# The projection stage of a cross-attention and feed-forward kernel, rebuilt: order of the transposes, place of the sums, weight pieces, context blocks

## The chip, the cores and the metric

One core of a Trainium2 chip. The metric is the device time of one execution in microseconds (us). Engines are named as in the profile: TensorE (PE, with its weight loads PEld), VectorE (DVE), ScalarE (ACT), GpSimd (POOL) and SyncE (SP), which here only issues transfers.

## The reference

```python
# x (1, 4096, 512), ctx (1, 3202, 1024), W_in (512, 512), w1 (512, 2048), w2 (2048, 512), all float32
h  = rmsnorm(layernorm(x), g_res) @ W_in.T + b_in
hp = rmsnorm(ctx, g_init)[:, :512]
s  = scan(hp)                    # s[i] = A' * s[i-1] + exp(-0.001) * hp[i], a first-order recurrence
plug = clip(cumsum(boundary_mask) - 1, 0, 3201)    # boundary_mask from cumsum(mask)
x  = x + h + s[plug]
y  = layernorm(x)
x  = x + gelu(y @ w1 + b1) @ w2 + b2
```

Everything is float32. The kernel keeps that accuracy by splitting each matmul operand into a high and a low part of type float32r and taking three products (high by high, low by high, high by low).

## The kernel before

x is cut into 32 tiles of 128 rows; four tiles make a group (8 groups). There are two stages.

**The projection stage** makes x1 = x + h for each tile and stores it to DRAM (x1_dram). For tile t, `tile_stats` (DVE) takes mean and variance, `tile_scale` (POOL) makes scale and bias, `tile_norm` (ACT) writes the normalized rows to `na`, `transpose_first` (PE) puts four 128x128 transposes into one of two PSUM banks `t_bank`, `tile_high` (ACT) and `tile_low` (DVE) split them into `h_hi` and `h_lo` (two buffers each), `project` (PE) makes twelve 128x512 matmuls into one of four banks `acc`, `tile_add` (DVE) adds x and writes to one of two buffers `xb`, and SP stores `xb`. PE's order is: transposes of tile t+1, projection of tile t. x arrives in eight buffers `xa`, six tiles ahead. `tile_add` waits until the store of the tile two before has landed (`xb_stored`, line 934).

The context is handled in seven blocks of 512 rows. Three of them (NA = 3) are handled in the projection stage, one in each span of eight tiles: SP loads both halves (1 MB each), ACT takes squares (`squares`), POOL makes the scale (`context_scale`) and multiplies by g_init (`times_g_init`), ACT scales the rows (`scale_rows`), DVE scans over four rows (`scan_row`), a small banded product on PE (`carry`) carries the state across partitions, DVE adds it (`add_carry`), and SP stores the block into `table` in DRAM (`store_block`). The mask is turned into row numbers (`plug`) by DVE and PE in the first span.

The weights w1 (four chunks of 128 rows of K) and w2 (four chunks) are loaded whole, chunk by chunk, by ACT and SP (1 MB each). ACT makes `w_hi` (line 678), POOL `w_lo` (`low_weights`, line 478), in 128x512 pieces. The last pieces are made after the projection stage.

**The feed-forward stage (FFN)** handles group by group. For group g, POOL has gathered s[plug] by an indirect transfer into `x_next` on top of x1 + b_in (`add_bias`, `add_context`, lines 494 and 499); DVE takes statistics (`second_stats`) and normalizes (`second_norm`, line 1062), PE transposes (`transpose_second`, line 825), ACT and DVE split (`transposed_high`, `transposed_low`), all for group g+1 during the last steps of group g. The 16 steps m of a group are on PE: `ffn1(g, m)` (12 matmuls), then `ffn2(g, m-2)` (12 matmuls). A step's gelu is on ACT (h_hi and g_f32), its split on DVE. Groups 0 to 3 also handle context blocks 3 to 6. The preparation of group 0 is the end of the projection stage.

Each engine runs its own program in order; semaphores are all that links them. The order inside an iteration is written out by hand.

Of the kernel before, what the change touches and what calls it, by code (L numbers as in the profile page):

```python
# [30 lines left out]
P = 128  # L31
# [8 lines left out]
PT = 8  # L40
NPAIR = NT // PT
AHEAD = PT - 2
LEAD = 2
# [5 lines left out]
NA = 3  # L49
# [48 lines left out]
def xattn_ffn(nc, x, ctx, mask, w_in, b_in, g_res, g_init, w1, b1, w2, b2, out):  # L98
# [4 lines left out]
    w1_v = w1.rearrange("(k p) n -> k p n", p=P)  # L103
# [6 lines left out]
    with es:  # L110
# [28 lines left out]
        win_hi = place("win_hi", [P, K, D], F32R, offset=xt_at)  # L139
        win_lo = place("win_lo", [P, K, D], F32R, offset=xt_at + 8 * KB)  # L140
# [15 lines left out]
        xa = place("xa", [P, PT, D], F32, offset=w_hi_at + 6 * WC * 4)  # L156
# [15 lines left out]
        ch_all = place("ch_all", [P, R, D], F32, offset=n_rows_at)  # L172
        scan_in = place("scan_in", [P, R, D], F32, offset=w_lo_at + 7 * WC * 4)
        scan_out = place("scan_out", [P, R, D], F32, offset=w_lo_at + 6 * WC * 4)
        xb = place("xb", [P, 2, D], F32, offset=x_cur_at)
        na = place("na", [P, 2, D], F32, offset=x_cur_at + 4 * KB)
# [14 lines left out]

        st_a = sb("st_a", [P, PT, 6])
        mv_a = sb("mv_a", [P, PT, 2])
        va_a = sb("va_a", [P, PT])
        ra = sb("ra", [P, PT])
        na_bias = sb("na_bias", [P, PT])
# [34 lines left out]
        acc = [bank(f"acc{i}") for i in range(TI)]  # L231

# [5 lines left out]
        xa_loaded = [sem(f"xa_loaded{i}") for i in range(PT)]  # L238
        xb_stored = [sem(f"xb_stored{i}") for i in range(2)]
        w_loaded = [sem(f"w_loaded{i}") for i in range(WCH)]  # L240
        cl_loaded = sem("cl_loaded")
        ch_all_loaded = sem("ch_all_loaded")
# [31 lines left out]
        w_lo_done = sem("w_lo_done")  # L274
        w2_ready = sem("w2_ready")
        sq_done = sem("sq_done")
# [23 lines left out]
        def _(sp):  # L300
            sp.dma_start(xa[:, 0, :], x_v[0, :, 0, :]).then_inc(xa_loaded[0], 16)
# [8 lines left out]
            for t in range(1, AHEAD):  # L310
                sp.dma_start(xa[:, t, :], x_v[t // TI, :, t % TI, :]).then_inc(xa_loaded[t], 16)

            def load_rows(b, dst, cols, loaded):

                if isinstance(b, int) and b == 0:
                    p = ZEROS // R
                    n = R - ZEROS % R
                    sp.dma_start(dst[p:p + 1, R - n:R, :], ctx_v[0:n, cols].rearrange("(p j) d -> p j d", p=1))\
                        .then_inc(loaded, 16)
                    sp.dma_start(dst[p + 1:P, :, :], ctx_v[n:BLK - ZEROS, cols].rearrange("(p j) d -> p j d", j=R))\  # L320
                        .then_inc(loaded, 16)
                else:
                    rows = ctx_v[bass.ds(block_start(b), BLK), :].rearrange("(p j) d -> p j d", j=R)
                    sp.dma_start(dst, rows[:, :, cols]).then_inc(loaded, 16)

            def load_low_half(b):

                load_rows(b, cl[:], slice(0, D), cl_loaded)

            def load_high_halves(b):  # L330

                load_rows(b, ch_all[:], slice(D, DG), ch_all_loaded)

            def load_high_half(b, j):

                wait_apart(sp, sq_done, R * b + j - 1)
                rows = ctx_v[bass.ds(block_start(b), BLK), :].rearrange("(p j) d -> p j d", j=R)
                sp.dma_start(ch[:, j % 2, :], rows[:, j, D:DG]).then_inc(ch_loaded[j % 2], 16)
# [6 lines left out]
            def tile(h, t, more=True):  # L345

                h, t = h + t // PT, t % PT
                if not isinstance(h, int) or PT * h + t > 0:
                    wait_apart(sp, acc_read, PT * h + t)
                    v = (t - 1) % PT  # L350
                    g = 2 * h + (t - 1) // TI
                    sp.dma_start(x1_dram[g, :, v % TI, :], xb[:, v % 2, :]).then_inc(xb_stored[v % 2], 16)
                if more:
                    u = (t + AHEAD) % PT
                    g = 2 * h + (t + AHEAD) // TI
                    sp.dma_start(xa[:, u, :], x_v[g, :, u % TI, :]).then_inc(xa_loaded[u], 16)

            def load_late_weights(c):

                sp.dma_start(w_raw[:, c, :].rearrange("p (m n) -> p m n", m=4), w2_v[c - 4, :, :, :])\  # L360
                    .then_inc(w_loaded[c], 16)

            def span(h, last=False):
                first = isinstance(h, int) and h == 0
                for s in range(PT - LEAD if last else PT):
                    if s == 7 and not first:
                        store_block(h - 1, scan_out)
                    if s == 5 and last:
                        store_block(h - 1, scan_in)
                    tile(h, LEAD + s, more=not last)  # L370
                    if s == 0 and not last:
                        if first:
                            wait_apart(sp, zeroed, 2)
# [832 lines left out]
```

## Time and profile before

| | us |
|---|---|
| median of 3 runs | 908.57 |
| lowest, highest | 906.12, 911.9 |
| span of the profiled execution | 907.9 |
| that execution's own device time | 909.6 |
| PE busy in the span | 847.1 (93%) |
| DVE, ACT, POOL busy | 329.9, 292.7, 285.2 |

Busy time is summed over the instructions of an engine; for PE the ends are modelled and matmuls overlap, so the distance between the starts of matmuls says more than the duration of one. Times of the trace are counted from the start of the span. An instruction's row may end in the idle time of its engine before it and in the one that ended that idle time.

### The profile page before, as it was taken

The numbers are of one execution on the slowest core, as the hardware profiler recorded it, in microseconds if no ns is written. First come the engines' busy times: TensorE is split into PE (matmuls) and PEld (weight loads), VectorE is DVE, ScalarE is ACT, GpSimd is POOL, SyncE is SP. The second block draws the span as 40 slices with busy tenths as digits, with TensorE's granted clock in tenths as the row PEclk, the third lists the DMA queues.
The fourth block names the chain that finished last, engine by engine and source line by source line (L and its number), as shares of the span: only waits on it lengthen the run. The fifth ranks groups of instructions, "written<-read, shape, count | busy, mean of one in ns | idle before, by whom it ended". The sixth has DMA issues, their size and how long they took to land.

```text
span 907.9 us, 11322 instructions
## 1 busy us (share of the span) xinstructions
PE 847.1 (93%) x3781; PEld 696.2 (77%) x3781; DVE 329.9 (36%) x531; ACT 292.7 (32%) x505; POOL 285.2 (31%) x323
## 2 busy tenths in 40 slices
PE   5688787379999999999999999999999999999998
PEld 4576665268888888888888888888888888888886
DVE  4766565351444144314431443213221322232112
ACT  3375562034323431343234322223222222222221
POOL 4275564491822070217022603400430043002000
PEclk8898997879999999999999999999999999999999
DMA  7956745432124131403140312300220032001001
GB/s 221 300 194 209 238 148 181 100 128 70 24 67 132 55 45 46 162 23 46 45 162 23 46 45 93 47 1 1 92 46 0 0 102 36 0 0 47 1 1 46
DMA packets 34414, 73.14 MB, mean 81 GB/s; under 512 B 5548, under 2 KB 6572, under 8 KB 31984
## 3 DMA queue, kind: packets, MB, share of 16 engines
q1 hardware_dynamic: 25124, 57.34, 18.8%
q0 software_dynamic: 4608, 8.39, 6.3%
q10 hardware_dynamic: 4656, 7.09, 2.5%
q8 instruction: 13, 0.21, 0.1%
q14 instruction: 13, 0.11, 0.0%
HBM read 48.92 MB, written 23.89 MB: 80 GB/s over the span
## 4 chain that ended last, share of the span: by engine, by line
PE 81%; DMA 7%; DVE 4%; POOL 4%; issue 2%; ACT 1%; ACTq 1%; SPq 1%; POOLq 0%; DVEq 0%
PE acc L781 13%; PE acc L782 13%; PE acc L783 13%; PE h_bank L781 13%; PE h_bank L782 13%; PE h_bank L783 13%; DMA x_part<-xb 3%; PE t_bank L825 2%; DMA x_next<-scan_table,idx 1%; DMA x_next<-x_part 1%; DMA g_init_b<-in_L_xattn_g_init_dram 1%; DMA xa<-in_x_dram 1%; POOL cl L505 1%; DVE h_lo L926 1%; POOL x_next L494 1%
## 5 line engine op out<-in xcount | busy, mean ns | idle before, releaser
L1146 DVE TENSOR_TENSOR h_lo<-g_f,h_hi 128x512 fp32r<-128x512 f32 x128 | 111.9, 874 | 441.1 <-ACT g_f L744 441.1
L742 ACT ACTIVATE h_hi<-h_bank,b_c 128x512 fp32r<-128x512 f32 x128 | 88.3, 690 | 453.9 <-PE h_bank L783 453.9
L781 PE MATMUL h_bank<-xt_hi,w_hi 128*128 128x512 f32 x512 | 200.7, 392 | 1.5 <-DVE xt_lo L1067 1.5
L781 PE MATMUL acc<-w_hi,h_hi 128*128 128x512 f32 x512 | 200.0, 391 | 0.0
L782 PE MATMUL h_bank<-xt_lo,w_hi 128*128 128x512 f32 x512 | 199.9, 390 | 0.0
L783 PE MATMUL h_bank<-xt_hi,w_lo 128*128 128x512 f32 x512 | 199.8, 390 | 0.0
L783 PE MATMUL acc<-w_hi,h_lo 128*128 128x512 f32 x512 | 199.4, 389 | 0.0
L782 PE MATMUL acc<-w_lo,h_hi 128*128 128x512 f32 x512 | 199.2, 389 | 0.0
L781 PEld LDWEIGHTS h_bank<-xt_hi,w_hi 128*128 128x128 f32 x512 | 96.6, 189 | 21.7 <-ACT xt_hi L725 1.9
L783 PEld LDWEIGHTS h_bank<-xt_hi,w_lo 128*128 128x128 f32 x512 | 96.6, 189 | 20.1
L782 PEld LDWEIGHTS h_bank<-xt_lo,w_hi 128*128 128x128 f32 x512 | 96.6, 189 | 19.8
L783 PEld LDWEIGHTS acc<-w_hi,h_lo 128*128 128x128 f32 x512 | 96.1, 188 | 20.0
L781 PEld LDWEIGHTS acc<-w_hi,h_hi 128*128 128x128 f32 x512 | 96.1, 188 | 20.0 <-issue 0.3
L782 PEld LDWEIGHTS acc<-w_lo,h_hi 128*128 128x128 f32 x512 | 96.2, 188 | 19.8
L584 POOL TENSOR_TENSOR x_cur<-x_next,b_b 128x512 f32<-128x512 f32 x32 | 47.8, 1524 | 159.1 <-DMA out_dram<-x_cur 158.9
L744 ACT ACTIVATE g_f<-h_bank,b_c 128x512 f32<-128x512 f32 x128 | 87.4, 683 | 2.1 <-DVE h_lo L1146 2.1
L781 PE MATMUL acc<-win_hi,h_hi 128*128 128x512 f32 x128 | 58.6, 458 | 9.5 <-DVE h_lo L926 9.5
L494 POOL TENSOR_TENSOR x_next<-x_next,b_in_b 128x512 f32<-128x512 f32 x32 | 54.1, 1690 | 22.8 <-DMA x_next<-x_part 22.2
L499 POOL DMA_INDIRECT x_next<-scan_table,idx x32 | 53.3, 1666 | 25.1 <-POOL x_next L494 25.1
L509 POOL TENSOR_SCALAR va_b<-mv_b 128x4 f32<-128x4 f32 x8 | 1.6, 195 | 172.9 <-DVE mv_b L1053 172.9
L782 PE MATMUL acc<-win_lo,h_hi 128*128 128x512 f32 x128 | 55.3, 432 | 0.0
L783 PE MATMUL acc<-win_hi,h_lo 128*128 128x512 f32 x128 | 54.8, 428 | 0.0
(133 smaller groups left out, 694.8 us busy)
## 6 DMA issues: line engine op xcount, KB each, us to landing
xa<-in_x_dram SPq DMA_DIRECT2D x32, 256.0 KB, 5.9
x_part<-xb SPq DMA_DIRECT2D x32, 256.0 KB, 3.7
x_next<-x_part SPq DMA_DIRECT2D x8, 1024.0 KB, 4.8
out_dram<-x_cur SPq DMA_DIRECT2D x32, 256.0 KB, 2.1
w_raw<-in_L_ffn_w_dram ACTq DMA_DIRECT2D x6, 1024.0 KB, 9.8
cl<-in_ctx_dram SPq DMA_DIRECT2D x6, 1024.0 KB
ch<-in_ctx_dram SPq DMA_DIRECT2D x16, 256.0 KB, 2.7
scan_table<-cl SPq DMA_DIRECT2D x4, 992.0 KB
```

The source lines that it names most:

```text
L494: step(pool.tensor_tensor(v, v, b, ALU.add))
L499: pool.indirect_dma_start(x_next[:, i, :], None, rows, bass.IndirectOffsetOnAxis(ap=idx[:, i:i + 1].bitcast(U32), axis=0), compute_op=ALU. ...
L505: pool.tensor_tensor(cl[:, j, :], cl[:, j, :], g_init_b[:], ALU.mult).then_inc(g_scaled, 1)
L584: ins = pool.tensor_tensor(x_cur[:, i, :], x_next[:, i, :], b2_b[:], ALU.add)
L742: act.activation(h_hi[:, m % HB, :], h_bank[m % 2][:], ACT.Gelu, bias=b1_c[:, m:m + 1])
L744: act.activation(g_f32[:], h_bank[m % 2][:], ACT.Gelu, bias=b1_c[:, m:m + 1]).then_inc(gelu_done, 1)
L781: nc.tensor.matmul(dst, a_hi, b_hi, start=first, stop=False)
L782: nc.tensor.matmul(dst, a_hi, b_lo, start=False, stop=False)
L783: return nc.tensor.matmul(dst, a_lo, b_hi, start=False, stop=final)
L825: ins = nc.tensor.transpose(t_bank[i % 2][:, k * P:(k + 1) * P], n_rows[:, i, k * P:(k + 1) * P], ident[:])
L926: dve.tensor_tensor(h_lo[:, t % 2, :], t_bank[t % 2][:], h_hi[:, t % 2, :].bitcast(F32), ALU.subtract).then_inc(t_lo, 1)
L1146: dve.tensor_tensor(h_lo[:, m % HB, :], g_f32[:], h_hi[:, m % HB, :].bitcast(F32), ALU.subtract).then_inc(h_split, 1)
```

## The change

- **Transposes two tiles ahead.** PE's order becomes: transposes of tile t+2, projection of tile t. The transposes use four banks (`t_bank` 0 and 1, `acc` 2 and 3), the projections only `acc` 0 and 1. `h_hi` and `h_lo` have four buffers, the normalized rows go to `n_rows` (four). The loops over spans are written out, all 32 tiles.
- **Sums in place.** `tile_add` writes into the tile of x; x has 16 buffers (`xa_even`, `xa_odd`), loaded 13 tiles ahead. SP stores from there, and waits for the store of tile t-3 before it loads tile t+13 over it. `xb` is gone.
- **Statistics six tiles ahead**, scales for two tiles in one set of four operations (`scales`).
- **Weights.** w1 comes in four pieces of 512 columns, all K, instead of four chunks of 128 rows; w2 as before. w1 pieces 0 and 1 and w2 chunk 0 are split in the projection stage; w2(1), w1(2), w2(2), w1(3), w2(3) by ACT in group 0 of the FFN, with the low parts on POOL, those of w1(3) and w2(3) on DVE. Five of the eight loads move to SP, at t = 25, 27, 29 and after the last tile.
- **Context.** Two blocks (NA = 2) in the projection stage; blocks 2 to 6 in FFN groups 0 to 4, at earlier steps of a group (squares from step 1, scan at 7, carry at 8, store after 9). The block's table entries are then gathered in the same group.
- **FFN preparation.** Group 0's four gathers come one after the other at t = 23; its norms at t = 28 to 30, its transposes at t = 30 and 31. In each group the second statistics are at steps 12 and 13, all four norms at step 14.
- **Order at the start.** The clears of `cl` and `ch_all` stand behind the scales of tile 0, `band` is made later, the mask's preparation is spread over t = 0 to 12. g_init, b_in and b2 are loaded ahead of b1 and of the weights.

The core of the diff (waits and unchanged neighbours cut):

```diff
-PT = 8
-NPAIR = NT // PT
-AHEAD = PT - 2
-LEAD = 2
+XR = 16
+SR = 4
-NA = 3
+NA = 2
...
+        xa_even = place("xa_even", [P, XR // 2, D], F32, offset=xt_at)
+        xa_odd = place("xa_odd", [P, XR // 2, D], F32, offset=w_hi_at + 6 * WC * 4)
+        first_bank = [t_bank[0], t_bank[1], acc[2], acc[3]]
...
+            for t in range(1, 6):
+                load_tile(t)
+            wait_apart(sp, zeroed, 2)
+            load_first_rows(ch_all, slice(D, DG), ch_all_loaded)
+            load_first_rows(cl, slice(0, D), cl_loaded)
+            for t in range(6, XR):
+                load_tile(t)
+            for t in range(NT):
+                if t > 0:
+                    store_x1(t - 1)
+                if t >= 3:
+                    wait_x1(t - 3)
+                    if t - 3 + XR < NT:
+                        load_tile(t - 3 + XR)
+                if t == 4:
+                    sp.dma_start(cl_next[:], block_rows(1)[:, :, 0:D]).then_inc(cl_next_loaded, 16)
+                if t == 8:
+                    wait_apart(sp, sq_done, R)
+                    sp.dma_start(ch_all[:], block_rows(1)[:, :, D:DG]).then_inc(ch_all_loaded, 16)
+                if t == 15:
+                    store_block(0, cl)
+                if t == 17:
+                    wait_apart(sp, table_stored, STORED + 16)
+                    load_low_half(NA)
+                if t == 19:
+                    sp.dma_start(x_next[:], x1_dram[0, :, :, :]).then_inc(x_next_loaded, 16)
+                if t == 22:
+                    store_block(1, cl_next)
+                    load_high_half(NA, 0)
+                    load_high_half(NA, 1)
+                if t == 25:
+                    wait_apart(sp, table_stored, STORED + 16 * 2)
+                    load_w2(1)
+                if t == 27:
+                    load_w1(2)
+                if t == 29:
+                    load_w1(3)
...
# POOL
+            scales(0, 1)
+            pool.memset(cl[:], 0.0).then_inc(zeroed, 1)
+            pool.memset(ch_all[:], 0.0).then_inc(zeroed, 1)
+            scales(1, 1)
+            scales(2, 2)
...
+            for t in range(NT):
+                if t % 2 == 0 and t + 6 < NT:
+                    scales(t + 6, 2)
+                if t == 3:
+                    pool.wait_ge(small_loaded, 16 * 4)
...
+                if t == 23:
+                    wait_apart(pool, table_stored, STORED + 16 * 2)
+                    for i in range(TI):
+                        add_context(0, i, 2)
...
# PE
-                if not isinstance(n, int) or n >= TI:
-                    pe.wait_ge(acc_read, n - TI + 1)
+                if t >= 2:
+                    pe.wait_ge(acc_read, t - 1)
...
+            transpose_first(0)
+            transpose_first(1)
+            for t in range(NT):
+                if t + 2 < NT:
+                    transpose_first(t + 2)
...
+                if t == 30:
+                    transpose_second(0, 0)
+                    transpose_second(0, 1)
+                if t == 31:
+                    transpose_second(0, 2)
+                    transpose_second(0, 3)
+                project(t)
...
# DVE
-                if not isinstance(n, int) or n >= 2:
-                    dve.wait_ge(xb_stored[t % 2], 16 * (PT // 2 * h + t // 2))
-                dve.tensor_tensor(xb[:, t % 2, :], acc[t % TI][:], xa[:, t, :], ALU.add).then_inc(acc_read, 1)
+                dve.tensor_tensor(xa(t), acc[t % 2][:], xa(t), ALU.add).then_inc(acc_read, 1)
...
+            for t in range(NT):
+                if t > 0:
+                    tile_add(t - 1)
+                if t + 2 < NT:
+                    tile_low(t + 2)
+                if t == 0:
+                    mask_parts()
+                if t + 6 < NT:
+                    tile_stats(t + 6)
+                if t == 2:
+                    mask_positions()
+                if t == 3:
+                    mask_places()
+                    one_hots_q()
+                if t == 4:
+                    one_hots_p(0, MJ // 2)
+                if t == 5:
+                    one_hots_p(MJ // 2, MJ)
...
+                if t == 31:
+                    for i in range(TI):
+                        transposed_low(0, i)
+            tile_add(NT - 1)
```

## Rows read from the trace of the kernel before

**Rows 1.** The page's slices: PE's busy tenths in 40 equal slices.

```profile
PE   5688787379999999999999999999999999999998
```

**Rows 2.** Stage table: stretch, length, busy us (instructions) by engine, PE clock, DMA share, GB/s.

```profile
0.00:191.00 191.00, 133.47 (x586) 104.92 (x587) 111.82 (x223) 84.04 (x141) 101.53 (x172) 0.85 0.63 194
63.00:76.00 13.00, 12.93 (x64) 10.44 (x64) 8.92 (x17) 8.18 (x10) 6.56 (x15) 1.00 0.73 254
191.00:196.00 5.00, 5.00 (x16) 3.95 (x16) 0.00 (x0) 1.09 (x2) 5.00 (x5) 0.67 0.83 276
```

**Rows 3.** Timeline of PE: start us, us, instruction, [idle before, what ended it].

```profile
15.34 0.79 PE L781 MATMUL acc<-win_hi,h_hi 128*128 128x512 f32 x1 [1.16 <-DVE h_lo L926]
...
20.46 0.60 PE L777 MATMUL t_bank<-ident,na 128*128 128x128 f32 x4
...
33.66 1.11 PE L777 MATMUL t_bank<-ident,na 128*128 128x128 f32 x4 [5.39 <-ACT na L630]
...
63.07 0.65 PE L777 MATMUL t_bank<-ident,na 128*128 128x128 f32 x4 [2.89 <-DVE h_lo L926]
...
72.72 0.60 PE L777 MATMUL t_bank<-ident,na 128*128 128x128 f32 x4
...
181.65 1.12 PE L825 MATMUL t_bank<-ident,n_rows 128*128 128x128 f32 x4 [12.94 <-DVE n_rows L1062]
...
190.61 0.77 PE L781 MATMUL h_bank<-xt_hi,w_hi 128*128 128x512 f32 x1 [1.50 <-DVE xt_lo L1067]
```

**Rows 4.** Table of waits: who waited for whom, us in total, times, longest.

```profile
DVE xb L935 <- DMA x_part<-xb: 16.9, 5, 4.9
...
POOL va_a L467 <- DMA g_init_b<-in_L_xattn_g_init_dram: 10.6, 1, 10.6
```

**Rows 5.** Chain of work that ended last, stretch 0 to 230: start us, us, what.

```profile
67.93 9.00 DMA x_part<-xb
...
93.60 13.47 DMA x_part<-xb
...
164.72 12.80 DMA x_next<-scan_table,idx
```

**Rows 6.** Timeline of DVE, and two of its groups by line (count, busy, mean ns).

```profile
26.27 0.17 DVE L990 CAST fa<-ia 128x26 f32<-128x26 int32 x1
...
28.43 0.18 DVE L1001 CAST pos_q<-ib 128x26 f32<-128x26 int32 x1
...
68.50 0.69 DVE L926 TENSOR_TENSOR h_lo<-t_bank,h_hi 128x512 fp32r<-128x512 f32 x1 [0.40 <-ACT h_hi L644]
...
70.61 0.71 DVE L941 SCALAR_TENSOR_TENSOR scan_in<-scan_in 128x512 f32<-128x512 f32 x1
...
269.06 1.00 DVE L1062 TENSOR_SCALAR n_rows<-x_next,mv_b,rb 128x512 f32<-128x512 f32 x2
...
L945 DVE CAST l_hi<-scan_in 128x512 fp32r<-128x512 f32 x3 | 3.9, 1291 | 0.0
L1005 DVE TENSOR_TENSOR oh_p<-pos_p,iota_p 128x1664 bf16<-128x1664 f32 x2 | 3.8, 1881 | 0.0
```

**Rows 7.** Groups of POOL by line, 0 to 191 us: count, busy, mean ns, idle before.

```profile
L478 POOL TENSOR_TENSOR w_lo<-w_raw,w_hi 128x512 fp32r<-128x512 f32 x15 | 20.0, 1401 | 0.0
L469 POOL TENSOR_TENSOR ra<-va_a,neg_half 128x1 f32<-128x1 f32 x32 | 17.7, 552 | 4.8 <-POOL va_a L467 0.8
...
L478 POOL TENSOR_TENSOR w_lo<-w_raw,w_hi x8 | 10.2, 1281 | 0.0
L499 POOL DMA_INDIRECT x_next<-scan_table,idx x4 | 6.7, 1666 | 3.3 <-POOL x_next L494 3.3
...
L461 POOL MEMSET cl<- 128x2048 f32 x1 | 1.8, 1804 | 0.2 <-POOL band L456 0.2
```

**Rows 8.** Timeline of ACT with its issues (ACTq), and its weight copies by line.

```profile
18.55 3.85 ACTq L674 DMA_DIRECT2D b_in_b<-in_L_xattn_b_in_dram  x1
...
L678 ACT ACTIVATE w_hi<-w_raw (+1 forms) x7 | 13.3, 1901 | 0.0
```

**Rows 9.** DMA issues, 0 to 192 us: count, median us from issue to landing.

```profile
x_next<-scan_table,idx POOLq DMA_INDIRECT x4, 5.5
```

More of the change, by code:

```diff
@@ L391, in _ @@
-            sp.sem_inc(table_stored, STORED)
-            for t in range(LEAD):
-                tile(0, t)
-            span(0)
-            with sp.Fori(1, NPAIR - 1) as h:
-                span(h)
-            span(NPAIR - 1, last=True)
-            wait_apart(sp, acc_read, NT)
-            sp.dma_start(x1_dram[NG - 1, :, TI - 1, :], xb[:, 1, :]).then_inc(xb_stored[1], 16)
-            wait_apart(sp, table_stored, STORED + 16 * NA)
-            load_late_weights(7)
-            for s in xb_stored:
-                wait_apart(sp, s, 16 * NT // 2)
@@ L412, in group @@
+            store_x1(NT - 1)
+            load_w2(2)
+            load_w2(3)
+            for t in range(NT - SR, NT):
+                wait_x1(t)
+            def group(g, scan, more, prep):
                 if prep:
@@ L551, in _ @@
-            tile_scale(0, 0)
-            tile_scale(1, 1)
-            tile_scale(2, 2)
-            tile_scale(3, 3)
-            pool.wait_ge(small_loaded, 16 * 4)
-            span(0)
-            with pool.Fori(1, NPAIR - 1) as h:
-                own.looped(h, 1, 2 * PT + 3)
-                span(h)
-            own.left(NPAIR - 2)
-            span(NPAIR - 1, last=True)
-            for q in range(4):
-                low_weights(4, q, 6, w2_ready)
-            low_weights(3, 2, 6, w_lo_done)
@@ L704, in _ @@
-            tile_norm(0, 1)
-            tile_high(0, 0)
-            first_loads(0)
-            tile_high(1, 1)
-            tile_norm(0, 2)
-            first_loads(1)
-            span(0)
-            act.wait_ge(counted, 1)
-            for c in range(1, 6):
-                act.wait_ge(w_loaded[c], 16)
-            with act.Fori(1, NPAIR - 1) as h:
-                own.looped(h, 1, R)
-                span(h)
-            own.left(NPAIR - 2)
-            span(NPAIR - 1, last=True)
-            act.sem_inc(gelu_done, CREDIT)
@@ L751, in group @@
                     transposed_high(g + 1, 3)
-            with act.Fori(0, NB - NA) as g:
-                own.looped(g, 0, R)
+            group(0, True, True)
+            with act.Fori(1, NB - NA) as g:
+                own.looped(g, 1, R)
                 group(g, True, True)
-            own.left(NB - NA)
+            own.left(NB - NA - 1)
             with act.Fori(NB - NA, NG - 1) as g:
@@ L890, in group @@
                         ffn2(g, m - LAG)
[L891 removed]
+                    if scan and m == 8:
                         carry(NA + g, t_bank[0][:])
@@ L1122, in _ @@
-            tile_low(0, 0)
-            tile_stats(0, 2)
-            tile(0, 1)
-            mask_positions()
-            span(0)
-            with dve.Fori(1, NPAIR - 1) as h:
-                own.looped(h, 1, PT + R)
-                span(h)
-            own.left(NPAIR - 2)
-            span(NPAIR - 1, last=True)
-            for i in range(TI):
-                second_norm(0, i)
-            tile_add(NPAIR - 1, PT - 1)
-            dve.wait_ge(h_used, NT)
-            for i in range(TI):
-                transposed_low(0, i)
+            tile_stats(0)
@@ L1139, in group @@
+            tile_add(NT - 1)
             def group(g, scan, prep):
+                first = isinstance(g, int) and g == 0
                 for m in range(M):
```

716 lines of the change are left out of this document (353 added, 363 removed).

## The prediction

> **What bounds the kernel now.** I read the page's slices first. TensorE (PE) is full in the last thirty of them; all holes lie in the first nine [rows 1]. The stage table gives them a size: in the first 191 us PE is busy for 133.5, at a mean granted clock of 0.85 [rows 2]. The feed-forward stage (FFN) begins with the h_bank matmul at 190.61 us [rows 3] and runs to the end of the span, 907.9: 717.3 us in which PE waits for nothing worth naming. So the change is worth what it does to the first 190.6 us.
>
> What would they cost without waits? The transposes that open a tile start at 63.07 and, three tiles on, at 72.72 [rows 3]: 3.22 us a tile, of which twelve matmuls at 0.23 are 2.76 and the transposes 0.46. 32 tiles are 103 us, and the first product begins at 15.34 [rows 3]. Some 70 us are therefore waiting, low clock and tail. The table of waits and the chain name them:
> - A sum waits for a store. DVE xb waits 16.9 us in five waits [rows 4], and the chain shows single stores landing after 9.00 and 13.47 us [rows 5]. They share SyncE's (SP) queue with the 1 MB transfers of the context blocks, and only two xb buffers lie between them and PE.
> - GpSimd (POOL) waits 10.6 us for g_init before the scales of tile 4 [rows 4], so PE waits for that tile's norm: after a tile that ended near 28 the next transpose comes at 33.66, 5.39 us late and at low clock [rows 3].
> - The tail. The fourth gather of group 0 lands 12.80 us after its issue [rows 5], and PE waits 12.94 us for the norms [rows 3].
>
> **The change, part by part.** T(t) is the moment at which PE turns to tile t, which now opens with the transposes of tile t+2.
>
> *Sums into the tile of x.* xb and its wait are gone. A slot of x is reused only after 16 tiles, and SP issues loads 13 tiles ahead for statistics that run 6 ahead: 7 tiles, 22.5 us, of cover against the worst store seen (13.47). I price the store waits at nothing; without that cover they are the 16.9 us again. What comes next is the sum itself: acc has two banks instead of four, so project(t+1) waits for the add of tile t-1. That add can start when project(t-1) ends and must be done before project(t+1) starts: 3.22 us plus 0.4 of transposes, less 0.6 for the add, so some 2.9 us of lateness are allowed.
>
> *The budget of VectorE (DVE).* One tile costs it h_lo, statistics, aggregate and add: 68.50 to 70.61, 2.11 us [rows 6]. That leaves 1.1 us a tile for lumps. Eleven small mask operations take 2.4 us (26.27 to 28.6 [rows 6]): one such set at t=2, one with the one-hot q (half an one-hot p, 1.0) at t=3, and one-hot p twice 1.88 at t=4 and 5 [rows 6]. Lateness runs 1.3, 3.6, then +0.8 and +0.8; what exceeds 2.9 is PE waiting: 0.7+0.8+0.8. Block 0 at t=11 is three scan rows (0.7, as at 70.61), a cast of 1.29 [rows 6] and a subtract of 0.7: 4.1 us; then the plug (six small ones, 1.4) and two carry steps of 1.3: +0.1, +0.4, +0.2, +0.2. Block 1's lumps (t=17 to 21) stay under. In sum 3 us. Bound below: 0. Bound above: no lateness allowed at all. Then 32 x 2.11, 36 for all lumps and second statistics and 0.4 us a tile of waiting for ACT's copy are 116 us against PE's 103: 13 us. In [rows 6] a tile with a scan row in it still kept to 3.2 us, so I stay near the low end.
>
> *Two tiles ahead: the start.* project(0) now stands behind transpose_first(2), thus behind the statistics of tiles 2 and 3, their scales and the norm of tile 2. POOL clears cl and ch_all (1.80 us each [rows 7]) after scales(0), so norm(1) ends near 14.2; h_hi 0.6, h_lo 0.6 and two statistics of 0.85 make 17.1. Scales for two tiles: four small operations and a power; one power of one column takes 0.55 [rows 7], of two columns between that and 1.1, I take 0.7; with the hops 1.9: 19.0. Norm 0.8, first transposes: project(0) at about 20.7, 5.4 us later than now (bounds: 18, if the clears and scales overlap better, and 23). Its 12 matmuls follow a long idle, so at 1.2 GHz like those from 15.34 to 20.46: 5.1 us [rows 3]. In return the gap before 33.66 goes: g_init is issued first, and POOL asks for it only at t=3, near 32 us. One ACT issue took 3.85 us right behind the many small pieces of b1 [rows 8]; b1 now goes last, in front of a weight load. Between 0 and 3.85 us; the two tiles of lead hide it, I take 0.
>
> *Weights in pieces.* 8 subtracts of w1 and 4 of w2 stay in the stage; at 1.28 to 1.40 us [rows 7] that is 16 us of POOL, and with scales, context and gathers it stays under 80 of the 103. ACT's copies of 1.90 us [rows 8] at t=7, 14 and 18 go with high (0.6) and norm (0.8): 3.3 us against 3.22. w2(1), w1(2), w1(3), w2(2) and w2(3) are split in group 0 of the FFN, where ffn1 and ffn2 of a step take 24 x 0.23 = 5.5 us. POOL there: 6 us for x_cur, 4 x 1.4 for w2(1), the context, and 4 x 1.4 for w1(2) until 39 us into the stage; needed at step 8, 44. Bias and w2(2) until 50; needed behind ffn1(10), 58. DVE's subtracts at steps 10 and 11 are done 6 us after ffn1(10), needed 8 after. Price 0; uncovered, each late chunk costs up to 5 us.
>
> *Two blocks instead of three first.* 2 MB of loads, 1 MB of store and 8 us of DVE leave the stage. In each FFN group all norms move to step 14: a norm takes 0.50 [rows 6] and stands between h_lo and transposes that PE is ready for at about that time: 0 to 0.5 us for each of 7 groups; 0.3 makes 2. The FFN no longer starts at the low clock (granted 0.67 from 191 to 196 [rows 2]), which gives 5 x 0.33 = 1.7 back. The FFN stays at 717.3.
>
> *The tail.* Block 1 is ready near T(22)+1. Its 1 MB store: 194 GB/s at a share of 0.63 [rows 2] is 308 GB/s at full share, 3.4 us, with issue and receipt 5. Four gathers back to back, 1.67 each [rows 7], end at T(22)+12.8; landing takes 5.5 at the median [rows 9]: T(27)+2.2, where DVE wants the last one at T(27)+2.4. No slack. Bounds: 0, and 10 if store or gather meet the delays of [rows 5]; most landings are near the median, I take 2. At t=31 the second pair of second transposes asks for xt_lo, which DVE makes after project(30) and its add: 0.6+0.7+0.1, then 0.7, less one transpose: 1.7 us.
>
> **Sum.** 20.7 start + 5.1 first tile + 31 x 3.22 = 99.8 + 4.4 for counts, mask totals, two carries (three matmuls each) and four transposes + 3 DVE + 1.7 + 2 tail = 136.7 us, against 190.6. With 717.3: a span of 854.0. The median of the runs, 908.57, lies 0.7 above the profile's span, so **855 us**.
>
> **Rivals.**
> - *As summed* (0.57): a pitch of 3.2 to 3.4 us; own range 845 to 864.
> - *The transfers crowd the tail* (0.22). For it: the stage still moves some 33.5 MB (191 us at 194 GB/s are 37 today), 109 us at 308 GB/s of its 130. The table store, the gathers and three weight loads meet at t=22 to 29, and POOL scales tiles 30 and 31 only after it has issued the gathers. Against: no x loads are left after t=18. 8 to 18 us more: 863 to 873. The Trainium skill (DMA: Bandwidth & Descriptors, "Queues, rings and completion order") says that an engine's semaphore write lands only after its earlier writes of all queues; the late stores of [rows 5] agree.
> - *DVE becomes the bound* (0.14). 10 to 13 us more than summed: 860 to 871.
> - *A weight chunk is late in group 0* (0.04): 5 to 20 us, 860 to 875.
> - *The clock stays low* (0.03), the other side. If DVE's short delays kept PE at 1.2 GHz throughout, a tile would be 12 x 0.43 + 1.1 = 6.2 us, the stage 20.7 + 198 + 8 = 227, the end 944. Slower begins at a pitch of 5.1. For it: 0.85 granted today, and 33.66. Against: 1.00 in the stretch of full tiles [rows 2]. The Trainium skill (TensorE: Matmul & The Clock Gate, "What's actually happening") calls the throttled clock the default that activity lifts; 15.34 and 33.66 agree.
>
> **The numbers.** The range runs from a start of 18 with nothing for DVE and tail (847), less 4 for terms that I rounded up (843), to the crowded tail with half of DVE's upper bound (880). About 1% is what a measurement tells from no change. Faster 0.95, within 1% 0.02, slower 0.03: only the last rival ends above.
>
> **What will show it.** First h_bank matmul near 137 us; transposes every 3.2 to 3.4 us from t=6 to t=29; no DVE wait on a store; clock 1.00 after 26 us; an FFN of 717. Wrong if PE waits for DVE's adds at most tiles, if st_b waits over 3 us for a gather, or if PE waits inside group 0.

## The result: the changed kernel is 2% slower

| | before | after |
|---|---|---|
| median of four runs, us | 909.1 (906.12 to 911.9) | 926.97 (925.03 to 929.68) |
| span of the profiled execution, us | 907.9 | 926.8 |
| first product (PE acc) | 15.34 | 20.76 |
| start of the FFN (first h_bank product of group 0) | 190.61 | 167.18 |
| from there to the end | 717.3 | 759.6 |

The ratio of the medians is 1.0199, with an interval of 1.0154 to 1.0244: the kernel did get slower, but whether by more or by less than 2% stays open. The forecast was 855 us. The projection stage did become shorter, by 23.4 us and not by 53.9. The FFN, whose time I had left as it was, became 42.3 us longer. 42.3 - 23.4 is the 18.9 us by which the two spans differ.

The slices of the page show both. First the row of PE, then the group of instructions of the page in which PE's new wait stands (busy time, mean ns of one, idle time just before and what ended it):

```profile
PE   3988895998799998999799979998999999999998
...
L831 PE MATMUL t_bank<-ident,n_rows 128*128 128x128 f32 x128 | 20.6, 312 | 30.1 <-DVE n_rows L1063 28.5
```

In [rows 1] the last thirty slices were full. Now a 7 or 8 comes back every fourth or fifth slice up to the twenty-eighth. The stage table puts sizes to it. Its columns are those of [rows 2]: the stretch and its length, PE, PEld, DVE, ACT and POOL, the granted clock, the DMA share and GB/s. The first row is group 0 of the FFN, the second is group 1, the third is a late group without a scan:

```profile
167.00:256.00 89.00, 80.64 (x350) 66.33 (x349) 32.76 (x45) 35.68 (x55) 37.88 (x31) 0.95 0.29 86
256.00:354.00 98.00, 91.73 (x405) 75.94 (x405) 29.50 (x45) 30.32 (x56) 26.70 (x23) 0.97 0.22 64
736.00:826.00 90.00, 89.93 (x405) 74.35 (x405) 21.67 (x36) 22.33 (x36) 19.34 (x15) 1.00 0.14 35
```

A group that scans a block lasts 98 us and a group that doesn't lasts 90, with the same 405 matmuls. The holes are at one place in each group. On PE's timeline (start, duration, line, tiles, count, and in brackets the wait before it) they stand at the transposes of the next group's rows, here of groups 1 and 2:

```profile
254.22 1.97 PE L831 MATMUL t_bank<-ident,n_rows 128*128 128x128 f32 x8 [5.48 <-DVE n_rows L1063]
351.89 1.96 PE L831 MATMUL t_bank<-ident,n_rows 128*128 128x128 f32 x8 [6.27 <-DVE n_rows L1063]
```

The other three are at 450.32 (6.40), 549.23 (6.64) and 645.30 (3.71). The table of waits tells what n_rows waited for. Each row is who waits for whom, the sum, the count and the longest wait:

```profile
PE t_bank L831 <- DVE n_rows L1063: 28.5, 5, 6.6
DVE st_b L1053 <- DMA x_next<-scan_table,idx: 63.0, 16, 13.3
POOL x_next L509 <- DMA scan_table<-cl: 160.0, 5, 34.0
```

Read upwards: POOL holds back the gathers until the store of the block has landed, DVE's statistics wait for the gathers, and PE waits for the norms. The chain of waits shows the store and the gather behind it (start and duration):

```profile
120.37 15.57 DMA scan_table<-cl_next
...
223.48 12.98 DMA scan_table<-cl
242.92 7.67 DMA x_next<-scan_table,idx
...
320.53 12.96 DMA scan_table<-cl
```

The store of one block takes 12.98 us. I had priced it at 5. And it takes this in the quiet FFN, with no crowd about it. The stage table of the stretch around the store of 223.48:

```profile
224.00:236.00 12.00, 12.00 (x55) 9.94 (x54) 6.20 (x10) 5.16 (x7) 0.00 (x0) 1.00 0.23 85
```

The share of the 16 DMA engines is 0.23 while nothing else of size moves, as if a quarter of them worked. The kernel before makes the same store, and its trace has nearly the same share in a stretch that the prediction did not use, just behind the issue at 260.9:

```profile
262.00:273.00 11.00, 11.00 (x54) 9.18 (x53) 3.60 (x8) 2.16 (x4) 1.24 (x2) 1.00 0.25 91
```

There the gathers of the next group did not need the block just stored, so nobody waited. The change moves two blocks out of the projection stage, and the gathers for group g+1 now need the block that group g makes. That puts the store on the path.

### The profile page after: what moved, and what is told of

Same layout as the page of the kernel before. It is cut to its first block, busy times and chain, and to the rows that moved or that the text cites. A ratio compares the mean times of both kernels' runs of the same rounds, so it can differ in the third digit from the quotient of the medians.

```text
span 926.8 us, 10866 instructions
## 1 busy us (share of the span) xinstructions
PE 852.5 (92%) x3781; PEld 701.8 (76%) x3781; DVE 320.3 (35%) x539; ACT 293.9 (32%) x506; POOL 265.6 (29%) x286
## 3 DMA queue, kind: packets, MB, share of 16 engines
q1 hardware_dynamic: 26756, 60.49, 19.3%
## 4 chain that ended last, share of the span: by engine, by line
PE 67%; DMA 15%; DVE 8%; POOL 5%; issue 3%; ACT 1%; DVEq 0%; ACTq 0%; POOLq 0%; SPq 0%
PE acc L788 11%; PE acc L790 11%; PE acc L789 11%; PE h_bank L788 10%; PE h_bank L789 10%; PE h_bank L790 10%; DMA scan_table<-cl 7%; DMA x_next<-scan_table,idx 5%; POOL x_next L509 3%; PE t_bank L831 2%; DMA scan_table<-cl_next 2%; DVE cl L957 1%; DVE st_a L929 1%; DMA x_part<-xa_even 1%; DVE cl L946 1%
## 5 line engine op out<-in xcount | busy, mean ns | idle before, releaser
L1146 DVE TENSOR_TENSOR h_lo<-g_f,h_hi 128x512 fp32r<-128x512 f32 x128 | 102.4, 800 | 425.6 <-ACT g_f L730 420.7
L788 PE MATMUL h_bank<-xt_hi,w_hi 128*128 128x512 f32 x512 | 203.0, 396 | 0.0
L790 PEld LDWEIGHTS h_bank<-xt_hi,w_lo 128*128 128x128 f32 x512 | 97.5, 190 | 20.7
L509 POOL DMA_INDIRECT x_next<-scan_table,idx x32 | 50.8, 1587 | 176.0 <-DMA scan_table<-cl 160.0
L831 PE MATMUL t_bank<-ident,n_rows 128*128 128x128 f32 x128 | 20.6, 312 | 30.1 <-DVE n_rows L1063 28.5
L504 POOL TENSOR_TENSOR x_next<-x_next,b_in_b 128x512 f32<-128x512 f32 x32 | 43.2, 1350 | 15.8 <-DMA x_next<-x_part 11.6
```

Source lines behind the costliest of these rows:

```text
L504: step(pool.tensor_tensor(x_next[:, i, :], x_next[:, i, :], b_in_b[:], ALU.add))
L509: pool.indirect_dma_start(x_next[:, i, :], None, rows, bass.IndirectOffsetOnAxis(ap=idx[:, i:i + 1].bitcast(U32), axis=0), compute_op=ALU. ...
L788: nc.tensor.matmul(dst, a_hi, b_hi, start=first, stop=False)
L790: return nc.tensor.matmul(dst, a_lo, b_hi, start=False, stop=final)
L831: ins = nc.tensor.transpose(t_bank[i % 2][:, k * P:(k + 1) * P], n_rows[:, i, k * P:(k + 1) * P], ident[:])
L1146: dve.tensor_tensor(h_lo[:, m % HB, :], g_f32[:], h_hi[:, m % HB, :].bitcast(F32), ALU.subtract).then_inc(h_split, 1)
```

## The experiments

**Theory A**: the block store is slow because its 124 partitions are spread over 4 of the 16 DMA engines, and this store is what PE waits for in the FFN and in the tail. **Rival B**: the four gathers in a row and all norms at step 14 are the cost (the chain behind the store is too long, however fast the store is). **Rival C**: the store is slow on its DRAM side, however it is cut.

The projection stage has a loss of its own. By the prediction's sum the transposes of tile 29 start near 115.2; they started at 133.73, 18.5 us later. **Theory D**: PE's carry, which stands ahead of the products of tiles 12 and 19 and waits for DVE, and the waits for norms near it have taken them. **Rival E**: VectorE is simply full.

Each quoted expectation was written before its run.

**1. The same store, cut where 16 engines share it.** 112 of the 124 partitions in one transfer, 12 in a second; the waits count 32 for a block and no longer 16. Bytes, order and dependences are the same.

```
     wait_apart(sp, block_ready, b + 1)
-    sp.dma_start(table[bass.ds(STEP * b, STEP), :].rearrange(...), src[HP:P, :, :]).then_inc(table_stored, 16)
+    sp.dma_start(table[bass.ds(STEP * b, 112 * R), :].rearrange(...), src[HP:HP + 112, :, :]).then_inc(table_stored, 16)
+    sp.dma_start(table[bass.ds(STEP * b + 112 * R, 12 * R), :].rearrange(...), src[HP + 112:P, :, :]).then_inc(table_stored, 16)
...
-    wait_apart(pool, table_stored, STORED + 16 * blocks)
+    wait_apart(pool, table_stored, STORED + 32 * blocks)
```

> The changed kernel with one edit: each block store of 124 partitions is issued as two, of 112 and of 12 partitions. Theory A (the store is slow, 12.95 us for 992 KB at a DMA share of 0.23, because a transfer of 124 partitions is spread over 4 of the 16 DMA engines, and since the gathers now wait for the block of their own group the wait reaches PE): the store lands in 4 to 6 us, POOL's wait for it shrinks by 8 us in each of groups 0 to 4, PE's waits for n_rows in the FFN (28.5 us) go to under 3, the FFN takes 718 to 722 instead of 759.6, the first stage loses about 8 of its 167; span 876 to 884. Theory B (the four gathers in a row and all norms at step 14 are what costs, the store only stands in front of them): the store may be faster, but PE still waits in each group; the FFN stays above 740, the span above 900. Theory C (the store is slow on its DRAM side, however it is cut): nothing changes, 925 to 929.

Measured: 879.6 us against 908.27, a ratio of 0.9679 (0.9657 to 0.9702). The FFN starts at 157.38 and lasts 720.7. From the timelines of SP and POOL, the issue of the store and the first gather that waited for it, and the stage table between them:

```profile
212.32 0.37 SPq L342 DMA_DIRECT2D scan_table<-cl  x1
...
217.77 1.68 POOL L511 DMA_INDIRECT x_next<-scan_table,idx  x1 [14.42 <-DMA scan_table<-cl]
...
212.50:217.50 5.00, 5.00 (x24) 4.14 (x23) 3.06 (x5) 3.08 (x3) 0.00 (x0) 1.00 0.61 203
```

From issue to gather it is 5.4 us, at a share of 0.61. PE has no wait for n_rows in the FFN any more. One edit of one transfer is worth 47.4 us, 38.9 of them in the FFN. A holds, and C falls.

**2. The dependence taken away, the store left slow.** The gathers read a table that is one block shorter. For the mask used here all rows asked for lie in it; for another mask this kernel would be wrong.

```
-    wait_apart(pool, table_stored, STORED + 16 * 2)
+    wait_apart(pool, table_stored, STORED + 16 * 1)
...
-        add_context(0, i, 2)
+        add_context(0, i, 1)
...
-    blocks = NA + g + 1 if scan else NB
+    blocks = NA + g if scan else NB
```

> The changed kernel, but each gather reads and waits for a table one block shorter (for this mask all rows asked for lie in it), so a block's store has a whole group of time, as in the kernel before. Theories A and C (the wait for the store is the cost): FFN 717 to 722, PE never waits for n_rows there, span 874 to 884. Theory B (gathers in a row, norms at step 14): FFN above 740 still, and the gathers land after 7.8 us at the median as now.

Measured: 884.62 us, ratio 0.9726 (0.9694 to 0.9758); FFN start 160.03, FFN 723.5. PE has no wait for n_rows in the FFN. This is as good as the fast store, within 5 us, though the FFN is 1.5 us above what I expected. So the 42 us need both the slow store and the dependence, and a fast store makes the dependence nearly free. B falls: gathers in a row and norms at step 14 are still there. Nor do the gathers still land after 7.8 us, as B said, but after 5.1.

**3. The cut store in the kernel before.** The same two lines, in the kernel before the change.

> The kernel before with the block stores cut in the same way. Theory A: its gathers wait for a store issued a group earlier, so the FFN stays at 717.3; the end of its first stage, where the third store and the weights met the fourth gather (12.80 us), may gain 0 to 8 us: span 900 to 908. Theory B and C: 907 to 909.

Measured: 894.42 us, ratio 0.9844 (0.9822 to 0.9867): 13.9 us faster, more than I expected. The FFN starts at 174.92 and lasts 716.8, so all of it is in the projection stage, which got 15.7 us shorter. The waits and PE's timeline say where:

```profile
DVE xb L937 <- DMA x_part<-xb: 6.9, 4, 3.7
...
165.98 1.11 PE L827 MATMUL t_bank<-ident,n_rows 128*128 128x128 f32 x4 [6.93 <-DVE n_rows L1064]
```

The waits of xb fell from the 16.9 of [rows 4] to 6.9, and the tail's wait from 12.94 [rows 3] to 6.93. These are 10.0 us on DVE and 6.0 us on PE; how much of DVE's 10.0 reached PE the waits do not tell. I had read the late stores of x (9.00 and 13.47 in [rows 5]) as a crowd on SP's queue. The block store had a good part in it: nothing else was changed here.

With the store cut in both kernels the change is worth 894.4 - 879.6 = 14.8 us: 17.5 in the projection stage, less 3.9 in the FFN (from the profiled executions, whose spans differ by 13.6; the rest is their distance from the medians).

**4. The carry behind the products.** With the slow store kept, PE multiplies the carry of block 0 after the products of tile 12 and that of block 1 after those of tile 19. ACT scales the rows of the block one tile later.

```
-                if t in (8, 9):
-                    scale_rows(0, cl, (2 * (t - 8), 2 * (t - 8) + 1))
+                if t in (9, 10):
+                    scale_rows(0, cl, (2 * (t - 9), 2 * (t - 9) + 1))
...
-                if t == 12:
-                    pe.wait_ge(band_ready, 1)
-                    carry(0, h_bank[0][:])
-                if t == 19:
-                    carry(1, h_bank[0][:])
...
                 project(t)
+                if t == 12:
+                    pe.wait_ge(band_ready, 1)
+                    carry(0, h_bank[0][:])
+                if t == 19:
+                    carry(1, h_bank[0][:])
```

> The changed kernel with the stores as they are, but PE takes the two carries of the first stage behind the projection of their tile instead of ahead of it, and ACT scales block 0's rows one tile later (t=9 and 10 instead of 8 and 9). Theory D (the 18 us that the first stage lost before its tail are PE's waits for the carry, 3.54 and 2.41 us, and for the norm of tile 12, 2.92 and 1.00, each followed by some 3 us at the low clock): transposes of tile 29 at 120 to 124 us instead of 133.7, span 914 to 919. Rival E (DVE is the bound, so a wait removed comes back as a later wait for an add): tile 29 at 131 or later, span 924 to 928.

Measured: 918.09 us, ratio 1.0089 (1.0057 to 1.012), FFN start 157.04, FFN 760.6. PE's timeline:

```profile
119.82 0.60 PE L783 MATMUL t_bank<-ident,n_rows 128*128 128x128 f32 x4
...
138.13 1.11 PE L783 MATMUL acc<-ident,n_rows 128*128 128x128 f32 x4 [14.94 <-ACT n_rows L638]
```

The transposes of tile 29 start at 119.82 where the changed kernel had them at 133.73. So 13.9 of the 18.5 us were the two waits for the carry, the wait for the scales and what they brought. But the tail's wait grew from 9.88 to 14.94: the gathers cannot come earlier than the slow store. D holds. E could at most explain the 4.6 us that are left.

**5. The store made slower.** The 124 partitions in two transfers of 62 and 62, each of which divides by 2 and not by 4. Same bytes, twice as many transfers as in the changed kernel, as in experiment 1.

```
+    sp.dma_start(table[bass.ds(STEP * b, 62 * R), :].rearrange(...), src[HP:HP + 62, :, :]).then_inc(table_stored, 16)
+    sp.dma_start(table[bass.ds(STEP * b + 62 * R, 62 * R), :].rearrange(...), src[HP + 62:P, :, :]).then_inc(table_stored, 16)
```

> The changed kernel with each block store cut into two of 62 partitions. Theory A (the number of engines of a transfer is the largest up to 16 that divides its partitions: 124 = 4 x 31 gives 4, 112 gives 16, 12 gives 12, 62 = 2 x 31 gives 2): cutting makes it slower, the store lands after about 25 us instead of 12.95, the DMA share during it is about 0.12, each of groups 0 to 4 gains another 12 us, span 985 to 1005. Theory F (a second transfer simply runs beside the first, whatever its shape): the store lands in 7 us, span 885 to 905. Theory C (the DRAM side limits): 925 to 929.

Measured: 986.21 us against 908.82, in a single execution; FFN start 182.40. From the chain of waits, the stage table and the table of waits:

```profile
237.83 21.91 DMA scan_table<-cl
...
238.00:259.00 21.00, 21.00 (x94) 17.42 (x93) 6.89 (x11) 6.87 (x9) 0.00 (x0) 1.00 0.12 48
...
PE t_bank L833 <- DVE n_rows L1065: 71.5, 5, 14.8
```

The share is 0.12 and PE waits 71.5 us instead of 28.5. Two transfers instead of one help nothing by themselves, so it is the partition count that decides, and F falls. The landing of 21.9 us is shorter than twice 12.95, and the five groups gained 8.5 us each and not 12.

**6. Both edits together**: the cut store and the carry behind.

> The changed kernel with the cut store (112 and 12 partitions) and with the carries behind the projection and block 0's scaling one tile later. Theory D (the waits before the tail are separate from the store's): the two gains add, about 9 us below the 879.6 of the cut store alone: 868 to 873, FFN start at 146 to 149 us. Rival E (the tail swallows it): 877 or more.

Measured: 869.68 us, ratio 0.9571 (0.9544 to 0.9599), FFN start 144.13. The FFN start is 2 us earlier than I expected. Together the edits give 57.3 us, while singly they gave 47.4 and 8.9, so the gains add. What is left before the FFN is mostly the tail. PE's timeline at tile 30:

```profile
125.88 1.12 PE L785 MATMUL acc<-ident,n_rows 128*128 128x128 f32 x4 [4.53 <-ACT n_rows L640]
```

**7. The gathers of group 0 in two pairs**, so that the scales of tile 30 don't stand behind four of them on POOL. **Theory G** says that this wait is POOL's queue; **rival H** says that the statistics of the gathered rows then wait for the later gathers and take its place.

```
                 if t == 23:
...
-                    for i in range(TI):
-                        add_context(0, i, 2)
+                    add_context(0, 0, 2)
+                    add_context(0, 1, 2)
+                if t == 25:
+                    add_context(0, 2, 2)
+                    add_context(0, 3, 2)
```

> As wide_behind, but POOL issues only two of group 0's gathers at t=23 and the other two at t=25, behind the scales of tiles 30 and 31. Theory G (what is left of the tail's stall is the norm of tile 30, queued on POOL behind four gathers: 3.78 us of wait and some 3 us of low clock): PE's wait for n_rows goes, 3 to 6 us below wide_behind. Rival H (the later gathers then hold up DVE's statistics): no change or 1 to 3 us more.

Measured: 870.36 us, the same as 869.68; FFN start 146.21 (144.13). From the timelines of PE and DVE:

```profile
124.41 0.66 PE L788 MATMUL acc<-ident,n_rows 128*128 128x128 f32 x4 [0.77 <-ACT n_rows L643]
...
125.23 0.69 DVE L1058 BATCH_NORM_STATS2 st_b<-x_next 128x6 f32<-128x512 f32 x1 [6.19 <-DMA x_next<-scan_table,idx]
128.27 0.77 PE L793 MATMUL acc<-win_hi,h_hi 128*128 128x512 f32 x1 [3.20 <-DVE xa_odd L945]
```

PE's wait for the norm fell to 0.77 as G says, but its gain did not come. DVE stands 6.19 us at a gather, and PE waits 3.20 for the add that is queued behind it. H was right in that nothing is gained, and wrong in its reason: this is the first gather, and in experiment 6 DVE stood at it for 6.07 us as well, behind PE's longer wait. The two later gathers cost DVE 0.15 and 0.65. From the transposes of tile 29 to the FFN it is 25.9 us here and 26.2 in experiment 6: the wait has only changed its name. The later FFN start was lost ahead of that.

**8. One tile ahead instead of two**, on top of experiment 1, to measure what the first part of the change gives.

```
             transpose_first(0)
-            transpose_first(1)
             for t in range(NT):
-                if t + 2 < NT:
-                    transpose_first(t + 2)
+                if t + 1 < NT:
+                    transpose_first(t + 1)
```

> The changed kernel with the cut store, but PE transposes one tile ahead, as before the change, all else (sums in place, banks, order of the other engines) kept. Theory I (two tiles ahead is what lets DVE's lumps pass without stopping PE): the first projection starts some 4 us earlier, but PE waits at the lumps of t=2 to 6, 11 to 14, 17 to 21; FFN start 8 to 18 us later than the 157.4 of the cut store alone, span 887 to 897. Theory J (the sums in place did all of it): FFN start 153 to 158, span 875 to 880.

Measured: 901.35 us, ratio 0.9914 (0.9894 to 0.9934), FFN start 177.07. PE's second tile of lead is worth 21.7 us here, more than I expected. The other engines keep an order written for two tiles, so a kernel arranged for one might lose less. The table of waits has them spread over several causes:

```profile
PE h_bank L790 <- DVE l_lo L952: 12.3, 2, 6.7
PE acc L790 <- DVE xa_odd L941: 6.7, 3, 5.0
PE acc L790 <- DVE xa_even L941: 5.7, 6, 2.2
```

**9. Clears and carry of the FFN moved**, on top of experiment 6. POOL clears its two tiles behind the scales of tile 1. PE's carry in the FFN comes one step later, since experiment 1 had shown a wait of 2.88 there at 203.95.

```
             scales(0, 1)
+            scales(1, 1)
             pool.memset(cl[:], 0.0).then_inc(zeroed, 1)
             pool.memset(ch_all[:], 0.0).then_inc(zeroed, 1)
-            scales(1, 1)
...
-                    if scan and m == 8:
+                    if scan and m == 9:
```

> wide_behind with two small edits: POOL clears cl and ch_all behind the scales of tile 1 instead of ahead of them, and in the FFN PE takes the carry at step 9 instead of 8 of a group. If the chain of the start is as summed (statistics, scales, norm, transposes), the first projection starts 1 to 2 us earlier than at 20.8; if the 2.9 us wait of group 0 is DVE's scan beside POOL's subtracts, it goes. Together 865 to 867 against 869.7. Rival: each reappears elsewhere (the context loads start 2 us later; the store of each block starts 2.7 us later and the gathers land late at step 13): 869 to 872.

Measured: 863.24 us against 908.76, ratio 0.9507 (0.949 to 0.9523). The FFN starts at 143.41 and lasts 717.6:

```profile
19.47 0.78 PE L790 MATMUL acc<-win_hi,h_hi 128*128 128x512 f32 x1
...
143.41 0.39 PE L790 MATMUL h_bank<-xt_hi,w_hi 128*128 128x512 f32 x1
```

The first product comes 1.1 us earlier than in experiment 6, and the FFN 0.7. The wait of group 0 is gone, and with it 6.0 of the 723.6 us that the FFN took there: more than I expected, since the clock had fallen behind that wait. The two edits were made in one run, but each shows in its own stage. This is the fastest version, 4.9% below the kernel before and 6.9% below the changed one.

## Why the prediction was wrong

The sum gave a span of 854.0. (The step from there to 855 set the median against the span of another execution; an execution's own time is 1.7 above its span, 909.6 against 907.9, which makes 856.) The span is 926.8. The 73 us between them are 42.3 in the FFN, 18.5 in the projection stage up to tile 29, and 12 in its tail.

**The term that failed: the price of the block store.** I took the mean rate of the whole stage at full share, 308 GB/s, for one transfer and wrote 5 us. A mean over many transfers says what 16 engines move together. It says nothing on how many of them one transfer gets. Per engine it comes near: 308 / 16 is 19.3 GB/s, and 992 KB on 4 engines at that rate are 13.2 us, where 12.96 to 12.98 were measured. That is in part luck, since not all of the landing is moving bytes. On half the engines (experiment 5) it took 21.9, 8.9 more; so by these two runs some 9 us of the 12.96 go with the number of engines and some 4 don't, which is an estimate. The store in the kernel before lay open at a share of 0.25 in 262:273. Pricing from that one quiet transfer, of the very kind that the change puts on the path, would have shown it.

**The step that was missing: "the FFN stays at 717.3".** I costed norms and weight chunks there, and named the gathers only in the projection stage's tail. The change makes the gathers of five groups wait for the block of the group itself. The chain is 13 us of store, gathers issued one behind the other, a landing of 7.7, statistics and norms. It ends 3.7 to 6.6 us after PE is ready. The waits sum to 28.5. Experiment 1 has the same instructions in its FFN and none of these five waits; against it the five groups, counted from transposes to transposes, lose 6.9, 7.9, 8.6, 9.1 and 6.3 us, which are the 38.9 but for rounding. The other 10.4 are the low clock, as behind the wait that ends at 351.89 (stage table):

```profile
352.00:356.00 4.00, 4.00 (x14) 3.52 (x15) 1.13 (x3) 0.00 (x0) 0.00 (x0) 0.50 0.00 0
```

In four of the groups PE works for a while at the lower clock behind its wait, and in group 0 also behind a wait of 2.88 for the carry at 213.75. The length of each such stretch times the clock that it lacked adds up to 11.0, an estimate close to the 10.4: 9.5 behind the waits for n_rows and 1.5 behind the carry. The wait for the carry itself is in experiment 1 too, 3.4 us above the 717.3; experiment 9 takes it away and has 717.6.

**The carry.** I counted the work of block 0 on DVE and let PE pass it by. But PE's carry stands in front of the products of tile 12, and everything behind it waits for l_lo too. PE's timeline of the changed kernel:

```profile
41.64 0.47 PE L788 MATMUL acc<-win_hi,h_hi 128*128 128x512 f32 x1 [2.16 <-DVE xa_even L940]
62.76 0.82 PE L783 MATMUL t_bank<-ident,n_rows 128*128 128x128 f32 x4 [2.92 <-ACT n_rows L638]
64.59 0.60 PE L824 MATMUL h_bank<-row_tot,tri 128*128 128x8 f32 x2 [1.00 <-DVE row_tot L1037]
70.38 0.60 PE L783 MATMUL t_bank<-ident,n_rows 128*128 128x128 f32 x4
77.71 0.77 PE L788 MATMUL h_bank<-l_hi,band_hi 128*128 128x512 f32 x1 [3.54 <-DVE l_lo L951]
106.19 0.50 PE L788 MATMUL h_bank<-l_hi,band_hi 128*128 128x512 f32 x1 [2.41 <-DVE l_lo L951]
```

The waits themselves sum to 12.0 us, against the 3 that I gave DVE's adds; 1.00 of them is the mask's count. Between 62.76 and 70.38 there is one tile: 7.62 us instead of 3.2. Its waits are 1.0, and the four small matmuls of the count take 0.9. The rest is the clock, which fell to 0.64 and 0.51 right behind the 2.92 (stage table):

```profile
62.00:66.00 4.00, 2.23 (x9) 1.79 (x10) 3.72 (x11) 3.97 (x9) 1.78 (x5) 0.64 0.55 209
66.00:70.00 4.00, 4.00 (x11) 3.09 (x10) 0.51 (x2) 0.48 (x2) 4.00 (x4) 0.51 0.37 131
```

In the second stretch PE is never idle, and yet it gets through 11 matmuls in 4 us. So the wait of 2.92 cost over 5: itself, and 7.62 - 3.2 - 1.0 - 0.9 = 2.5 of low clock in the next tile. The prediction knew the low clock only at the start and as a rival that would hold throughout. The 2.92 itself is a wait that moved: ACT waited 5.81 us for POOL's scales for the block's rows, and the norm of tile 12 was queued behind that on ACT:

```profile
60.19 1.33 ACT L657 ACTIVATE cl<-cl,rc 128x512 f32<-128x512 f32 x2 [5.81 <-POOL rc L491]
```

**The tail.** I gave it 2 us with a bound of 10, and it took 12 more than the 2. Here the rival "the transfers crowd the tail" had the right place and a size (8 to 18 us) that holds the 12, but mostly the wrong reason: the store takes 15.57 us here and 12.98 with nothing beside it, so a crowd accounts for 2.6 at most. POOL waited for it and issued the gathers late, and PE got the norm of tile 30, queued behind them, late (timelines of POOL and PE):

```profile
136.87 1.82 POOL L509 DMA_INDIRECT x_next<-scan_table,idx  x1 [7.04 <-DMA scan_table<-cl_next]
...
146.98 1.12 PE L783 MATMUL acc<-ident,n_rows 128*128 128x128 f32 x4 [9.88 <-ACT n_rows L638]
```

**What was right.** The first product came at 20.76 (predicted 20.7), and the first tile took 5.07 us (5.1). The start was right in its steps too, not only in the sum: the norm of tile 1, summed to end near 14.2, lets PE start its transposes at 14.29. PE's timeline:

```profile
20.76 0.78 PE L788 MATMUL acc<-win_hi,h_hi 128*128 128x512 f32 x1
25.83 0.60 PE L783 MATMUL acc<-ident,n_rows 128*128 128x128 f32 x4
...
111.32 0.60 PE L783 MATMUL acc<-ident,n_rows 128*128 128x128 f32 x4
133.73 0.60 PE L783 MATMUL t_bank<-ident,n_rows 128*128 128x128 f32 x4
...
163.36 1.22 PE L831 MATMUL t_bank<-ident,n_rows 128*128 128x128 f32 x8 [1.47 <-DVE xt_lo L1068]
```

From 111.32 to 133.73 are seven tiles, 3.20 us each as summed. The wait for xt_lo at t=31 is 1.47 (1.7). No DVE instruction waits for a store of x any more, and no chunk of weights is late in group 0. With the store cut and the carries moved the FFN takes 717.6, as predicted. The 863.24 us of experiment 9 lie 8 us above the forecast and inside its range, but that is another kernel. Its FFN starts at 143.41 and not at 136.7; among what the sum did not have is a wait of 4.60 for the norm of tile 30.

Of the other rivals, "DVE becomes the bound" did not come: between tiles 22 and 29 the pitch is PE's own. "The clock stays low" came only in short pieces, behind some of the waits. The other side of the forecast did come, through a mechanism that was not on my list.

**Open**: why the clock fell behind one wait and not behind another of the same length; why the kernel before gained 10.0 us at xb from the cut store, in which the order on SP's queue and the engines' queues aren't told apart; the 2.16 us at 41.64, for which there was no run; what holds the first gather of group 0 back in the tail once the store is fast.

## What to carry to other kernels

Price a transfer by the landing and the DMA share of that very transfer in a quiet stretch, never by the mean rate of a stage; a share near 4/16 beside a single transfer of 1 MB says that its partition count is badly cut. When a change puts a transfer between its producer and a consumer in the same round, walk the whole chain once in every stage in which it repeats, the ones that look finished too. On an engine with a queue in order, put an instruction that waits for another engine behind the work that is ready, and count with up to as much again for the clock at each wait of some 3 us on TensorE.

## What the runs showed of the hardware

- **The number of partitions decides how many DMA engines a transfer gets.** The same 992 KB in the FFN: 124 partitions in one transfer, 12.96 us at a share of 0.23; 112 and 12, 5.4 us from issue to the gather behind it, at 0.61; 62 and 62, 21.9 us at 0.12. Shares of 0.23 and 0.12 are close to 4/16 and 2/16. The Trainium skill (DMA: Bandwidth & Descriptors, "🔬 Why a DMA increments its semaphore by 16 and not by 1") says that a transfer is given the largest number of engines up to 16 that divides the slowest dimension of both its access patterns: that is 4 for 124, 16 for 112 and 2 for 62. All three traces agree with that rule. The landing itself is not in proportion to the engines: halving them took it from 12.96 to 21.9 us.
- **A short wait on TensorE can cost twice itself, or only itself.** After a wait of 2.92 us the granted clock was 0.64 and then 0.51, near the lower of its two levels, 1.2 GHz, for some 7 us, although PE had no idle time in the second half of it. But PE's wait of 2.88 us for the carry in group 0 was followed by 1.00 in experiment 1 and by 0.50 in experiment 6; without that wait (experiment 9) the FFN is 3.1 us shorter than the one and 6.0 shorter than the other. The wait's row on PE's timeline and the row of the stage table around or behind it, first of experiment 1, then of experiment 6:

```profile
203.95 0.50 PE L790 MATMUL t_bank<-l_hi,band_hi 128*128 128x512 f32 x1 [2.88 <-DVE l_lo L953]
204.00:208.00 4.00, 4.00 (x18) 3.29 (x19) 0.49 (x1) 0.30 (x1) 0.00 (x0) 1.00 0.00 0
...
190.70 0.80 PE L790 MATMUL t_bank<-l_hi,band_hi 128*128 128x512 f32 x1 [2.88 <-DVE l_lo L953]
190.00:194.00 4.00, 3.30 (x8) 2.66 (x9) 1.25 (x2) 0.00 (x0) 0.09 (x1) 0.50 0.00 0
```

- **Gathers landed later beside other transfers; coming together did little by itself.** The median landing was 7.8 us in the changed kernel, 6.5 with the cut store, 5.1 with the gathers a block shorter and 4.8 in the kernel before. The changed kernel and experiment 2 issue the four gathers of a group alike, each 0.30 us behind the last. In the changed kernel SP issues the loads of the next block just then, since they wait for the same store, and the DMA share is 0.86 from 237 to 250; in experiment 2 it is 0.58 from 288 to 300. No run changed that alone, so the cause is not shown.
